# One rotary rotation for queries and keys of a head, with the projections reordered and the reciprocals in PSUM

## The chip, the cores and the metric

The kernel runs on one core of a Trainium2 chip. The time is device microseconds (us) from launch to end of one execution. Three runs of the kernel before took 1827.94 to 1831.23 us, median 1830.76. The profile shown is of a further execution, of 1832.47 us; its span from the first to the last instruction is 1830.7 us. Times of day below are us from the start of that span. Engines: PE (TensorE), PEld (its weight loads), ACT (ScalarE), DVE (VectorE), POOL (GpSimd) and SP (SyncE), which here issues the DMAs of the attention stage.

## What is computed

A language-model block on 8 sequences (batches) of 512 tokens, 64 channels: token embedding with layer norm, attention with 16 heads, then a mixture of 8 experts. The change lies in the attention. Per batch and head:

```python
q  = concat([cq @ Wq_nope, rope(cq @ Wq_rope)])        # 512 queries; 64 of the columns are rotated
o1 = attn(q, k1, v1, causal)                           # compressed keys, the same rotation for all heads
ks = concat([sel @ Wsel_k[:, :32], rope(sel @ Wsel_k[:, 32:])])   # 128 selected tokens
o2 = attn(q, ks, vs)
kw = concat([x @ Wwin_k[:, :32], rope(x @ Wwin_k[:, 32:])])       # 512 tokens, window of 128
o3 = attn(q, kw, vw, window)
o  = g[0] * o1 + g[1] * o2 + g[2] * o3                 # then o @ Wproj
rope(x) = concat([xr * c - xi * s, xr * s + xi * c])   # xr, xi: halves of the 64 columns
```

## The kernel before, in words

The 512 tokens of a batch are four tiles of 128 tokens. Heads follow each other: 8 batches of 16, 128 in all. One head is a *turn* of four *units*, one unit for each tile of queries (`turn(...)` in the code of each engine, t = 0 to 3; the text counts the units from first to fourth). The engines run their own programs and meet at semaphores; no planner sets the order, it is written out by hand.

**PE** in unit t of turn h: a projection for a later head, if this unit has one; `scores` (L1356) of the unit three ahead, so that from the second unit on they belong to head h+1; `turn_probs` (L1381, L1388), which transposes the probabilities of the next unit; `values` (L1403) of this unit. The scores of head h+1 begin in the second unit and wait there for that head's transposed keys and queries (`k_turned`, `q_turned`). Projections: `k_proj(h+2)` in the first unit and `q_proj(h+2)` in the second (L1312, L1315, L1303). All projections write the one PSUM bank X, so each waits until ACT has emptied X of the one before (`x_wait`).

**ACT** empties X (`evac_k`, `evac_q`, both recorded at L576) at the head of the same units, then `take_hi` (L647: the high half of the transposed probabilities), then `probs` (L635: the exponentials). It works strictly in that order.

**DVE** takes `maxima` (L1008) and `take_lo` (L1018, the low half) in each unit, and at the end of a turn `combine`: reciprocals of the softmax sums (L1025, `rinv`, in SBUF), their product with the gates (L1027, `coef`), and the product with the branch outputs in PSUM bank O (L1030), which frees O for the values of the next head.

**POOL** prepares a head two ahead (`prepare`): `key` = rotation of 5 tiles of keys (four of the window, one of the selected tokens; 64 columns each) by two products (L424, L425) and a difference and a sum of half as many columns (L428, L429), then the split into a high and a low fp16 part (L457, L460); `query` = the same rotation of the 4 tiles of queries, from the same lines, and the split (L446, L449). A semaphore wait stands between products and difference, and between rotation and split. Then `low_values` (L480) and `branch_sum` (L473, L475) for the heads before. The rotation of the keys waits for `evac_k`, that of the queries for `evac_q`.

**SP** issues for each head the DMA transpose of the keys (L319, `kh<-kparts`) and then that of the queries (L328, `qh<-qparts`), each after its split.

So there is a round over two heads: projection of head h+2 in turn h, ACT, POOL, DMA, its scores in turn h+1, and the projection in turn h+2 after them.

**Between batches** turns 14 and 15 have projections of the next batch instead (the list `LEAD`, also through X), with single rotations on POOL, and `behind` fills the gap before the next batch's first turn: transposes of the attention output (L1479) that need POOL's last `branch_sum`. In turns 0 and 1 PE projects the output of the batch before (`project_rows`, L1416, into X as well) in the third and fourth unit; DVE adds it to the residual (`half_residual`, L1107) in the fourth, and PE waits at the end of the turn for that (`h_done`). In the last batch POOL also normalises rows for the experts in every second turn (`normalise`).

Of the kernel before, what the change touches and what calls it, by code (L numbers as in the profile page):

```python
# [23 lines left out]
K_ID, K_MASK, K_COS, K_SIN, K_IOTA, K_DESC, K_STK, K_END = 0, 128, 384, 704, 1024, 1152, 1164, 1228  # L24
# [8 lines left out]
def tower(nc, d, out):  # L33
# [5 lines left out]
    with ctx:  # L39
# [6 lines left out]
        def sem(name):  # L46
# [5 lines left out]
        cos5 = cst[:, K_COS:K_COS + 5 * ROPE].rearrange("p (t r) -> p t r", t=5)  # L52
# [97 lines left out]
        qs = [sb(f"qs{i}", [P, NT, QW]) for i in range(2)]  # L150
        kk = [sb(f"kk{i}", [P, 5, P]) for i in range(2)]
        work = big[:].rearrange("p a n -> p (a n)")
        NPR, NRT, NOB = 7 * P, 2 * 5 * ROPE, NT * 3 * VD
# [3 lines left out]
        rt = [work[:, 4 * NPR + i * NRT:4 * NPR + (i + 1) * NRT].rearrange("p (a t r) -> p a t r", a=2, t=5)  # L157
              for i in range(2)]
        obr = [work[:, 4 * NPR + 2 * NRT + i * NOB:4 * NPR + 2 * NRT + (i + 1) * NOB].rearrange("p (t k d) -> p t k d", t=NT, k=3)
               for i in range(2)]  # L160
        qparts = sb("qparts", [P, 2, NT, QW], fp16)
# [14 lines left out]
        rinv = sb("rinv", [P, NT, 3])  # L176
# [29 lines left out]
            "x_ready", "x_evac", "rope_tq", "rope_tk", "rope_q", "rope_k",  # L206
# [20 lines left out]
        ZT = PT[:, 7 * P:8 * P]  # L227
        TBANK = [X[0:C, :], S[0][0:C, 0:512]]
# [4 lines left out]
        LEAD = ["cq", "qp0", "sel", "k1", "kp0", "qp1", "kp1"]  # L233
        NX = (NH - 2) * 2 + len(LEAD)

        def x_index(p, kind):
            return 2 * p + ["kp", "qp"].index(kind)
# [130 lines left out]
        def _(g):  # L368
# [52 lines left out]
            def rope(src, tmp, part, done, tiles, n):  # L421

                v = src[:, 0:tiles, NOPE:HD]
                g.tensor_tensor(tmp[:, 0, 0:tiles, :], v, cos5[:, 0:tiles, :], ALU.mult)  # L424
                g.tensor_tensor(tmp[:, 1, 0:tiles, :], v, sin5[:, 0:tiles, :], ALU.mult).then_inc(part, 1)  # L425
                g.wait_ge(part, n)
                hf = ROPE // 2
                g.tensor_tensor(src[:, 0:tiles, NOPE:NOPE + hf], tmp[:, 0, 0:tiles, 0:hf], tmp[:, 1, 0:tiles, hf:ROPE], ALU.subtract)  # L428
                g.tensor_tensor(src[:, 0:tiles, NOPE + hf:HD], tmp[:, 0, 0:tiles, hf:ROPE], tmp[:, 1, 0:tiles, 0:hf], ALU.add).then_inc(done, 1)  # L429

            def rope_q(par, b, hh, x):

                g.wait_ge(s["x_evac"], x + 2)
                rope(qs[par], rt[0], s["rope_tq"], s["rope_q"], NT, b * NH + hh + 1)

            def rope_k(par, b, hh, x):
                g.wait_ge(s["x_evac"], x + 2)
                rope(kk[par], rt[1], s["rope_tk"], s["rope_k"], 5, b * NH + hh + 1)

            def split_query(par, b, hh):  # L440
                H = b * NH + hh
                g.wait_ge(s["rope_q"], H + 1)
# [8 lines left out]
            def split_key(par, b, hh):  # L451
                H = b * NH + hh
                g.wait_ge(s["rope_k"], H + 1)
# [8 lines left out]
            def query(par, b, hh, x):  # L462
                rope_q(par, b, hh, x)
                split_query(par, b, hh)

            def key(par, b, hh, x):
                rope_k(par, b, hh, x)
                split_key(par, b, hh)
# [12 lines left out]

            query(0, 0, 0, xbase(0) + x_lead("qp0"))
# [42 lines left out]
            def prepare(b, h, hh, par, rows=None):  # L525

                x = xbase(b) + h * 2
                key(par, b, hh, x + x_index(0, "kp"))
                query(par, b, hh, x + x_index(0, "qp"))
                if rows is not None:  # L530
                    normalise(rows, xn_b[:])
                low_values(1 - par, b, hh - 1)

            def heads(b, rows=False):
                prepare(b, 0, 2, 0, 0 if rows else None)
                with g.Fori(0, NH // 2 - 2) as hp:
                    prepare(b, hp * 2 + 1, hp * 2 + 3, 1)
                    branch_sum(0, b, hp * 2)
                    prepare(b, hp * 2 + 2, hp * 2 + 4, 0, hp + 1 if rows else None)
                    branch_sum(1, b, hp * 2 + 1)  # L540
                prepare(b, NH - 3, NH - 1, 1)
                branch_sum(0, b, NH - 4)
                branch_sum(1, b, NH - 3)
# [30 lines left out]
        def _(act):  # L574
# [83 lines left out]
            def turn(b, h, xb, p, last, nxt=None, rows=None):  # L658
# [3 lines left out]
                for t in range(NT):  # L662
                    u = p * NT + t
                    if t == 0 and last < 1:
                        evac_k(p, xb + x_index(0, "kp"), H + 1)
                    if t == 1 and last < 1:
# [3 lines left out]
                    if nxt is not None:  # L670
# [25 lines left out]
            def lead(i, nxt, H=None):  # L696
# [9 lines left out]
                elif kind[:2] == "qp":  # L706
                    evac_q(int(kind[2]), x, H)
                elif kind[:2] == "kp":
                    evac_k(int(kind[2]), x, H)

            def behind(b, nxt, U, first):
# [12 lines left out]
                probs(0, 0, b, U)  # L724
                if not first:
# [5 lines left out]
            for i in range(len(LEAD)):  # L731
# [5 lines left out]
            def heads(b, rows=False):  # L737
                with act.Fori(0, NH // 2 - 1) as hp:
                    for p in range(2):
                        turn(b, hp * 2 + p, xbase(b) + hp * 4 + p * 2, p, 0, rows=hp if rows and p == 1 else None)  # L740

# [53 lines left out]
        def _(dve):  # L795
# [225 lines left out]
            def combine(par, b, H):  # L1021
# [87 lines left out]
            def turn(b, H, p, last, nxt=None, rows=None, back=None):  # L1109

                U = H * NT
                for t in range(NT):
# [11 lines left out]
                    if back is not None and t == 3:  # L1124
# [105 lines left out]
        def _(pe):  # L1230
# [189 lines left out]
            def turn(h, H, xb, p, last, b=None, nxt=None, rows=None, back=None):  # L1420
# [3 lines left out]
                for t in range(NT):  # L1424
                    u = p * NT + t
                    if last < 1 and t == 0:
                        k_proj(h + 2, xb + x_index(0, "kp"))
                    if last < 1 and t == 1:
                        q_proj(h + 2, xb + x_index(0, "qp"))
                    if back is not None and t >= 2:  # L1430
                        project_rows(back, p * 2 + t - 2, xb + 2)
                    i = t if last == 1 else t + 4
                    if nxt is not None and i < len(LEAD):
# [15 lines left out]
                if back is not None:  # L1449
                    pe.wait_ge(s["h_done"], back * 2 + p + 1)  # L1450
# [21 lines left out]
            def behind(b, nxt, H, first):  # L1472
# [20 lines left out]
                scores(0, 0, 0, H * NT)  # L1493
                if not first:
# [19 lines left out]
            def heads(b, rows=False):  # L1514
                for p in range(2):
                    turn(p, b * NH + p, xbase(b) + p * 2, p, 0, rows=0 if rows and p == 1 else None, back=b - 1 if b > 0 else None)
                with pe.Fori(1, NH // 2 - 1) as hp:
                    for p in range(2):
                        turn(hp * 2 + p, b * NH + hp * 2 + p, xbase(b) + hp * 4 + p * 2, p, 0,
                             rows=hp if rows and p == 1 else None)  # L1520

# [20 lines left out]
            for kind in LEAD[2:]:  # L1542
# [130 lines left out]
def _constants():  # L1673
# [9 lines left out]
    for col, tab in ((K_COS, np.cos(ang)), (K_SIN, np.sin(ang))):  # L1683
        for t in range(5):
# [33 lines left out]
```

## Time and profile before

| | busy us | share of the span |
|---|---|---|
| PE | 1423.3 | 78% |
| PEld | 1150.3 | 63% |
| DVE | 1436.5 | 78% |
| ACT | 1225.4 | 67% |
| POOL | 1437.0 | 78% |
| span | 1830.7 | |
| this execution | 1832.47 | |
| median of three others | 1830.76 | |

The shares are means over the whole span. The first 230 us or so prepare embeddings and weights, the attention turns fill the stretch to 1751 us, and the experts the rest. TensorE's granted clock is at full speed (0.96 to 1.00) through the turns. A wait is put down to the semaphore that came last.

### The profile page before, as it was taken

The numbers are of one execution on the slowest core, as the hardware profiler recorded it, in microseconds if no ns is written. First come the engines' busy times: TensorE is split into PE (matmuls) and PEld (weight loads), VectorE is DVE, ScalarE is ACT, GpSimd is POOL, SyncE is SP. The second block draws the span as 40 slices with busy tenths as digits, with TensorE's granted clock in tenths as the row PEclk, the third lists the DMA queues.
The fourth block names the chain that finished last, engine by engine and source line by source line (L and its number), as shares of the span: only waits on it lengthen the run. The fifth ranks groups of instructions, "written<-read, shape, count | busy, mean of one in ns | idle before, by whom it ended". The sixth has DMA issues, their size and how long they took to land.

```text
span 1830.7 us, 62295 instructions
## 1 busy us (share of the span) xinstructions
PE 1423.3 (78%) x19368; PEld 1150.3 (63%) x19368; DVE 1436.5 (78%) x4989; ACT 1225.4 (67%) x3280; POOL 1437.0 (78%) x2126
## 2 busy tenths in 40 slices
PE   1041488888888888888888888888888888888778
PEld 0021377767777777777777776777767776766643
DVE  5747678887888788878887888888887888778845
ACT  0041277777777787778877777777767877777644
POOL 6775489877887899789987889788878997899610
PEclk9985699999999999999999999999999999999989
DMA  5110132223222322232222222222222222323200
GB/s 93 22 26 2 35 71 57 52 45 64 52 52 45 71 52 56 46 64 52 53 51 64 53 52 57 56 53 52 55 60 53 52 56 42 60 62 69 54 4 20
DMA packets 327634, 93.11 MB, mean 51 GB/s; under 512 B 321104, under 2 KB 323024, under 8 KB 327520
## 3 DMA queue, kind: packets, MB, share of 16 engines
q1 hardware_dynamic: 324448, 88.48, 24.9%
q0 software_dynamic: 3072, 3.15, 0.9%
q8 instruction: 66, 1.08, 0.2%
q14 instruction: 48, 0.39, 0.1%
HBM read 6.51 MB, written 1.05 MB: 4 GB/s over the span
## 4 chain that ended last, share of the span: by engine, by line
POOL 60%; issue 17%; DVE 10%; PE 8%; POOLq 2%; DMA 2%; ACT 1%; DVEq 0%; ACTq 0%; SPq 0%
POOL big L425 9%; POOL big L424 9%; POOL kparts L460 7%; POOL big L394 5%; POOL vh L480 4%; POOL qparts L446 4%; POOL kparts L457 4%; POOL kk L428 3%; POOL kk L429 3%; POOL qs L428 3%; POOL qs L429 3%; DVE S L1008 3%; POOL osum L473 2%; POOL qparts L449 1%; PE S L1356 1%
## 5 line engine op out<-in xcount | busy, mean ns | idle before, releaser
L635 ACT ACTIVATE big<-S,negm 128x128 f32<-128x128 f32 (+3 forms) x1536 | 577.4, 450 | 196.8 <-DVE negm L1008 195.7
L647 ACT ACTIVATE big<-PT 128x384 f16<-128x384 f32 (+3 forms) x1024 | 426.6, 455 | 150.7 <-PE PT L1381 112.2
L1018 DVE SCALAR_TENSOR_TENSOR big<-PT,big 128x384 f16<-128x384 f32 (+3 forms) x1024 | 472.1, 500 | 39.1 <-ACT big L647 26.3
L1008 DVE CUSTOM_DVE_ANT_0 S<-S,mask_c,unscale 128x128 f32<-128x128 f32 (+3 forms) x512 | 285.1, 557 | 182.8 <-PE S L1356 176.6
L1356 PE MATMUL S<-k1T,qh 128*128 128x128 f16 (+3 forms) x1536 | 296.8, 302 | 113.9 <-DMA qh<-qparts 98.0
L1356 PE MATMUL S<-kh,qh 128*128 128x128 f16 (+1 forms) x3072 | 323.3, 242 | 0.0
L1403 PEld LDWEIGHTS O<-vh,big 128*128 128x128 f16 x8064 | 272.7, 96 | 41.9 <-issue 14.3
L1403 PE MATMUL O<-vh,big 128*128 128x33 f16 x8064 | 283.3, 178 | 14.7 <-DVE big L1030 8.0
L1356 PEld LDWEIGHTS S<-kh,qh 128*128 128x128 f16 x3072 | 229.9, 99 | 56.0
L1388 PE MATMUL PT<-cst,big 128*128 128x128 f32 x1408 | 248.6, 281 | 16.8 <-DVE big L1018 15.1
L1381 PE MATMUL PT<-cst,big 128*128 128x128 f32 x1280 | 232.6, 281 | 19.1 <-DVE big L1018 17.4
L1008 DVE CUSTOM_DVE_ANT_0 S<-S,cst,kfix 128x256 f32<-128x256 f32 (+1 forms) x512 | 232.5, 454 | 0.0
L1008 DVE DVE_READ_ACCUMULATOR2_ANT negm<- 128x1 f32 x1536 | 217.0, 141 | 0.2
L1356 PEld LDWEIGHTS S<-k1T,qh 128*128 128x128 f16 x1536 | 113.4, 99 | 160.9 <-issue 109.4
L1388 PEld LDWEIGHTS PT<-cst,big 128*128 128x128 f32 x1408 | 162.9, 144 | 47.1 <-issue 40.8
L1008 DVE CUSTOM_DVE_ANT_0 S<-S,mask_c,kfix 128x128 f32<-128x128 f32 x512 | 181.4, 354 | 0.1
L1381 PEld LDWEIGHTS PT<-cst,big 128*128 128x128 f32 x1280 | 153.0, 144 | 38.2 <-DVE big L1018 19.1
L449 POOL TENSOR_TENSOR qparts<-qs,qparts 128x512 f16<-128x512 f32 x128 | 148.4, 1159 | 18.5
L460 POOL TENSOR_TENSOR kparts<-kk,kparts 128x480 f16<-128x480 f32 x128 | 140.9, 1101 | 18.6
L424 POOL TENSOR_TENSOR big<-kk,cst 128x320 f32<-128x320 f32 x128 | 110.3, 862 | 47.0 <-ACT kk L576 46.6
L1303 PE MATMUL X<-wqh,cqT 128*128 (+1 forms) x1536 | 114.5, 222 | 17.9 <-DVE cqT L960 14.8
L424 POOL TENSOR_TENSOR big<-qs,cst 128x256 f32<-128x256 f32 x128 | 93.7, 732 | 29.1 <-ACT qs L576 29.1
(298 smaller groups left out, 2399.7 us busy)
## 6 DMA issues: line engine op xcount, KB each, us to landing
lat_b<-lat_all SPq DMA_DIRECT2D x8, 448.0 KB, 3.1
qh<-qparts SPq DMA_TRANSPOSE x128, 3.0
kh<-kparts SPq DMA_TRANSPOSE x128, 3.4
xnT_all<-xnT_b SPq DMA_DIRECT2D x14, 128.0 KB, 2.5
xn_b<-xn_all SPq DMA_DIRECT2D x8, 128.0 KB, 2.9
xnT_b<-xnT_all SPq DMA_DIRECT2D x8, 128.0 KB, 2.4
out_dram<-h_all SPq DMA_DIRECT2D x8, 128.0 KB, 2.0
xn_all<-xn_b SPq DMA_DIRECT2D x7, 128.0 KB, 2.0
```

Source lines behind the costliest of these rows:

```text
L424: g.tensor_tensor(tmp[:, 0, 0:tiles, :], v, cos5[:, 0:tiles, :], ALU.mult)
L425: g.tensor_tensor(tmp[:, 1, 0:tiles, :], v, sin5[:, 0:tiles, :], ALU.mult).then_inc(part, 1)
L449: g.tensor_tensor(qparts[:, 1], qs[par][:], qparts[:, 0], ALU.subtract).then_inc(s["q_split"], 1)
L460: g.tensor_tensor(kparts[:, 1, :, NOPE:P], kk[par][:, :, NOPE:P], kparts[:, 0, :, NOPE:P], ALU.subtract).then_inc(s["k_split"], 1)
L635: last = nc.scalar.activation(pr[par][:, lo:lo + n], S[par][:, lo:lo + n], ACT.Exp, bias=negm[par][:, k:k + 1], scale=-1.0)
L647: last = nc.scalar.activation(pT[par][:, 0, lo:lo + n], PT[:, lo:lo + n], ACT.Copy, scale=PSCALE)
L1008: last = v.tensor_tensor_reduce(out=z, in0=z, in1=m, scale=unscale[:] if k == 0 else kfix[:], scalar=3.0e38, op0=ALU.add, op1=ALU.min, acc ...
L1018: v.scalar_tensor_tensor(pT[par][:, 1, lo:lo + n], PT[:, lo:lo + n], PSCALE, pT[par][:, 0, lo:lo + n], ALU.mult, ALU.subtract).then_inc(s[ ...
L1356: last = mm(z[:, lo:lo + n], qh[par][:, c, t * P:(t + 1) * P], keys[:, a, :], start=(c + a == 0), stop=(c == 1))
L1381: last = tp(PT[:, lo:lo + P], src[:, lo:lo + P], ident)
L1388: last = tp(PT[:, lo:lo + P], src[:, lo:lo + P], ident)
L1403: last = mm(o, w[:, c, blocks[i] * P:(blocks[i] + 1) * P], vh[p][:, a, v0 + i, :], start=(j == 0), stop=(j == len(parts) - 1))
```

## The change

The rotation of queries and keys of one head becomes one rotation of nine tiles. For that, the two live side by side (`qk`), the cosine table in the constants grows from five to nine tiles, and POOL copies a nine-tile sine table once at its start (two copies). PE projects the queries of head h+2 in the first unit of turn h and the keys of head h+3 in its fourth; the keys of head 2 of a batch come in `behind` (`kp2`, after the first scores). POOL waits for the queries alone before a head's rotation. ACT empties X in the same units. `project_rows` moves from the third and fourth to the second and third unit, `half_residual` to the third, and PE's wait for it ahead of the projection in the fourth. DVE writes the reciprocals into the free end of PSUM bank O. SP's program is not changed.

```diff
-K_ID, K_MASK, K_COS, K_SIN, K_IOTA, K_DESC, K_STK, K_END = 0, 128, 384, 704, 1024, 1152, 1164, 1228
+K_ID, K_MASK, K_COS, K_SIN, K_IOTA, K_DESC, K_STK, K_END = 0, 128, 384, 960, 1280, 1408, 1420, 1484
...
+        qk = [sb(f"qk{i}", [P, NT + 5, P]) for i in range(2)]
+        qs, kk = [q[:, 0:NT] for q in qk], [q[:, NT:NT + 5] for q in qk]
...
-        rinv = sb("rinv", [P, NT, 3])
+        rinv = O[:, NT * 3 * (VD + 1):NT * 3 * (VD + 2)]
...
-        LEAD = ["cq", "qp0", "sel", "k1", "kp0", "qp1", "kp1"]
+        LEAD = ["cq", "qp0", "sel", "k1", "kp0", "qp1", "kp1", "kp2"]
...
+            g.tensor_copy(sin9[:, 0:NT], sin5[:, 0:NT]).then_inc(s["sin_ready"], 1)
+            g.tensor_copy(sin9[:, NT:NT + 5], sin5).then_inc(s["sin_ready"], 1)
+            def rope(src, tmp, cos, sin, n):
+                v, hf = src[:, :, NOPE:HD], ROPE // 2
+                g.tensor_tensor(tmp[:, 0], v, cos, ALU.mult)
+                g.tensor_tensor(tmp[:, 1], v, sin, ALU.mult).then_inc(s["rope_t"], 1)
+                g.wait_ge(s["rope_t"], n)
+                g.tensor_tensor(src[:, :, NOPE:NOPE + hf], tmp[:, 0, :, 0:hf], tmp[:, 1, :, hf:ROPE], ALU.subtract)
+                g.tensor_tensor(src[:, :, NOPE + hf:HD], tmp[:, 0, :, hf:ROPE], tmp[:, 1, :, 0:hf], ALU.add).then_inc(s["rope"], 1)
...
-            def prepare(b, h, hh, par, rows=None):
-                x = xbase(b) + h * 2
-                key(par, b, hh, x + x_index(0, "kp"))
-                query(par, b, hh, x + x_index(0, "qp"))
+            def prepare(par, b, hh, x):
+                n = rope_count(b, hh, None)
+                g.wait_ge(s["x_evac"], x + 2)
+                rope(qk[par], rt9, cos9, sin9, n)
+                split_key(par, b, hh, n)
+                split_query(par, b, hh, n)
...
@@ ACT, turn @@
                     if t == 0 and last < 1:
-                        evac_k(p, xb + x_index(0, "kp"), H + 1)
-                    if t == 1 and last < 1:
                         evac_q(p, xb + x_index(0, "qp"), H + 1)
                     if t == 2 and last < 2:
                         high_values(1 - p, b, h + 1)
+                    if t == 3 and last < 1 and more:
+                        evac_k(1 - p, xb + x_index(0, "kp"), H + 2)
...
@@ ACT, behind @@
                 probs(0, 0, b, U)
+                lead(LEAD.index("kp2"), nxt, b * NH)
...
@@ DVE, combine @@
-                v.reciprocal(rinv[:].rearrange("p t k -> p (t k)").unsqueeze(2), o3[:, :, VD:VD + 1]).then_inc(s["coef_chain"], 1)
+                v.reciprocal(rinv.unsqueeze(2), o3[:, :, VD:VD + 1]).then_inc(s["coef_chain"], 1)
...
-                v.tensor_tensor(coef[:], rinv[:], bc(gate_all[:, ds(b, 1), :], [P, NT, 3]), ALU.mult).then_inc(s["coef_chain"], 1)
+                v.tensor_tensor(coef[:], rinv.rearrange("p (t k) -> p t k", k=3), bc(gate_all[:, ds(b, 1), :], [P, NT, 3]), ALU.mult).then_inc(s["coef_chain"], 1)
...
@@ DVE, turn @@
-                    if back is not None and t == 3:
+                    if back is not None and t == 2:
                         half_residual(back, p)
...
@@ PE, turn @@
                     if last < 1 and t == 0:
-                        k_proj(h + 2, xb + x_index(0, "kp"))
-                    if last < 1 and t == 1:
                         q_proj(h + 2, xb + x_index(0, "qp"))
-                    if back is not None and t >= 2:
-                        project_rows(back, p * 2 + t - 2, xb + 2)
+                    if back is not None and t in (1, 2):
+                        project_rows(back, p * 2 + t - 1, xb + 1)
+                    if back is not None and t == 3:
+                        pe.wait_ge(s["h_done"], back * 2 + p + 1)
+                    if last < 1 and t == 3 and more:
+                        k_proj(h + 3, xb + x_index(0, "kp"))
...
-                if back is not None:
-                    pe.wait_ge(s["h_done"], back * 2 + p + 1)
...
@@ PE, behind @@
                 scores(0, 0, 0, H * NT)
+                lead("kp2", b, nxt)
```

## Rows read from the trace of the kernel before

**Rows 1.** The page: the chain that ended last, by engine.
```profile
POOL 60%; issue 17%; DVE 10%; PE 8%; POOLq 2%; DMA 2%; ACT 1%; DVEq 0%; ACTq 0%; SPq 0%
```

**Rows 2.** Stretches: length, busy us of PE, PEld, DVE, ACT, POOL; clock, DMA.
```profile
264.02:384.46 120.44, 104.05 (x1560) 87.24 (x1558) 103.39 (x387) 96.69 (x255) 108.02 (x164) 0.99 0.27 52
...
1397.94:1519.71 121.77, 103.48 (x1558) 87.11 (x1556) 103.16 (x386) 96.63 (x255) 108.30 (x165) 0.99 0.28 54
1590.04:1724.06 134.02, 111.71 (x1629) 94.81 (x1629) 107.40 (x426) 97.91 (x278) 121.21 (x186) 0.99 0.32 63
```

**Rows 3.** Waits, 643.34 to 763.53 us: who for whom, total us, times, longest.
```profile
PE S L1356 <- DMA qh<-qparts: 14.2, 11, 1.4
...
POOL kparts L457 <- POOL kk L429: 2.8, 11, 0.3
```

**Rows 4.** Timeline, POOL, one head: start, us, instruction, [idle before <- releaser].
```profile
687.69 0.86 POOL L424 TENSOR_TENSOR big<-kk,cst 128x320 f32<-128x320 f32 x1
...
695.06 0.61 POOL L446 CAST qparts<-qs 128x512 f16<-128x512 f32 x1 [0.19 <-POOL qs L429]
695.82 1.16 POOL L449 TENSOR_TENSOR qparts<-qs,qparts 128x512 f16<-128x512 f32 x1
...
698.25 0.46 POOL L475 TENSOR_TENSOR o_b<-osum,big 128x128 f32 x1 [0.18 <-POOL osum L473]
698.66 0.86 POOL L424 TENSOR_TENSOR big<-kk,cst 128x320 f32<-128x320 f32 x1
```

**Rows 5.** Waits, 794 to 824 us (turns 0 and 1 of one batch).
```profile
POOL big L424 <- ACT kk L576: 5.3, 3, 2.6
...
PE X L1312 <- DVE h_all L1107: 2.2, 2, 1.3
```

**Rows 6.** Waits, 763 to 798 us (the edge between two batches).
```profile
POOL osum L473 <- DVE big L1030: 4.0, 1, 4.0
...
PE PT L1479 <- POOL o_b L475: 1.4, 1, 1.4
```

**Rows 7.** Groups by shape, POOL, whole run: count, busy us, mean ns, idle before.
```profile
L425 POOL TENSOR_TENSOR big<-kk,cst 128x320 f32<-128x320 f32 x128 | 110.4, 862 | 0.0
...
L425 POOL TENSOR_TENSOR big<-qs,cst 128x256 f32<-128x256 f32 x128 | 93.8, 733 | 0.0
...
L428 POOL TENSOR_TENSOR kk<-big 128x160 f32<-128x160 f32 x128 | 67.6, 528 | 10.0
...
L428 POOL TENSOR_TENSOR qs<-big 128x128 f32<-128x128 f32 x128 | 58.7, 458 | 10.0
```

**Rows 8.** Timeline, PE, the same head.
```profile
689.45 0.34 PE L1356 MATMUL S<-k1T,qh 128*128 128x128 f16 x3 [1.39 <-DMA qh<-qparts]
...
695.56 0.59 PE L1312 MATMUL X<-wkw,xh 128*128 x8
...
696.08 0.81 PE L1356 MATMUL S<-k1T,qh 128*128 128x512 f16 x3
...
698.15 0.91 PE L1303 MATMUL X<-wqh,cqT 128*128 x12
700.37 0.34 PE L1356 MATMUL S<-k1T,qh 128*128 128x128 f16 x3 [1.31 <-DMA qh<-qparts]
```

**Rows 9.** Timeline, ACT, the same head.
```profile
695.83 1.21 ACT L635 ACTIVATE big<-S,negm 128x384 f32<-128x384 f32 x3 [0.34 <-DVE negm L1008]
696.92 0.58 ACT L576 ACTIVATE kk<-X 128x480 f32<-128x480 f32 x1
```

**Rows 10.** The page: DMA issues, count, KB each, median us to landing.
```profile
lat_b<-lat_all SPq DMA_DIRECT2D x8, 448.0 KB, 3.1
qh<-qparts SPq DMA_TRANSPOSE x128, 3.0
kh<-kparts SPq DMA_TRANSPOSE x128, 3.4
```

**Rows 11.** DVE, lines L1027 and L1030, whole run: ns min/median/max.
```profile
L1027 DVE TENSOR_TENSOR coef<-rinv,gate_all x128: 170/602/739, 239.5 to 1750.5; 128x12 f32<-128x12 f32 x128
...
L1030 DVE TENSOR_TENSOR big<-O,coef x128: 556/558/560, 239.7 to 1750.7; 128x384 f32<-128x384 f32 x128
```

More of the change, by code:

```diff
@@ L656, in take_hi, with turn @@
                     last.then_inc(s["pT_hi"], 1)
-            def turn(b, h, xb, p, last, nxt=None, rows=None):
+            def turn(b, h, xb, p, last, nxt=None, rows=None, more=True):
                 H = b * NH + h
@@ L669, in turn @@
                         high_values(1 - p, b, h + 1)
-                    if nxt is not None:
+                    if t == 3 and last < 1 and more:
+                        evac_k(1 - p, xb + x_index(0, "kp"), H + 2)
+                    if nxt is not None and (last == 1 or t < 3):
                         lead(t if last == 1 else t + 4, nxt, b * NH + NH)
@@ L729, in behind @@
                 probs(2, 2, b, U + 2)
-            for i in range(len(LEAD)):
+            for i in range(LEAD.index("kp2")):
                 lead(i, 0)
@@ L737, in heads @@
             def heads(b, rows=False):
-                with act.Fori(0, NH // 2 - 1) as hp:
+                with act.Fori(0, NH // 2 - 2) as hp:
                     for p in range(2):
                         turn(b, hp * 2 + p, xbase(b) + hp * 4 + p * 2, p, 0, rows=hp if rows and p == 1 else None)
+                for p in range(2):
+                    turn(b, NH - 4 + p, xbase(b) + (NH - 4 + p) * 2, p, 0, rows=NH // 2 - 2 if rows and p == 1 else None, more=p == 0)
             def last_heads(b, nxt):
@@ L1418, in project_rows, with turn @@
                     last.then_inc(s["attn_psum"], 1)
-            def turn(h, H, xb, p, last, b=None, nxt=None, rows=None, back=None):
+            def turn(h, H, xb, p, last, b=None, nxt=None, rows=None, back=None, more=True):
                 U = H * NT
@@ L1516, in heads @@
                     turn(p, b * NH + p, xbase(b) + p * 2, p, 0, rows=0 if rows and p == 1 else None, back=b - 1 if b > 0 else None)
-                with pe.Fori(1, NH // 2 - 1) as hp:
+                with pe.Fori(1, NH // 2 - 2) as hp:
                     for p in range(2):
@@ L1520, in heads @@
                              rows=hp if rows and p == 1 else None)
+                for p in range(2):
+                    turn(NH - 4 + p, b * NH + NH - 4 + p, xbase(b) + (NH - 4 + p) * 2, p, 0,
+                         rows=NH // 2 - 2 if rows and p == 1 else None, more=p == 0)
             def hidden(b, chunks=(0, 1, 2, 3), between=None):
@@ L1541, in _ @@
             last.then_inc(s["rank_psum"], 1)
-            for kind in LEAD[2:]:
+            for kind in LEAD[2:LEAD.index("kp2")]:
                 lead(kind, 0, 0)
@@ L1682, in _constants @@
     ang = np.outer(np.arange(T, dtype=np.float32), f)
-    for col, tab in ((K_COS, np.cos(ang)), (K_SIN, np.sin(ang))):
-        for t in range(5):
+    for col, tab, n in ((K_COS, np.cos(ang), 9), (K_SIN, np.sin(ang), 5)):
+        for t in range(n):
             rows = tab[(t % NT) * P:(t % NT) * P + P]
```

73 lines of the change are left out of this document (36 added, 37 removed).

## The prediction

> **What bounds the kernel now.** I began with the chain of waits that ended last: 60% of it is POOL [rows 1], though POOL's busy share of the span is no larger than DVE's. Next I read the stretches. In each of the first seven batches eleven head periods, from the `combine` of head 2 to that of head 13, make one stretch; the seven sum to 846.7 us for 77 heads (first and last are shown), 11.00 us each; the last batch needs 134.02/11 = 12.18 [rows 2]. In these stretches POOL is busy for 108 of 120 us, and its waits are for nothing but itself (0.25 us a head between rotation and split), while PE stands 14.2 us in 11 heads waiting for transposed queries [rows 3]. So POOL runs its list without a pause, 698.66 - 687.69 = 10.97 us a head [rows 4], and the others follow. In the last batch POOL's busy share is as high [rows 2], with normalisations on top. It is otherwise in turns 0 and 1 of a batch, where POOL waits 5.3 us for the keys, and PE 2.2 us for the residual [rows 5], and at the edge between batches, where POOL waits for `combine` and PE for POOL's sum [rows 6].
>
> **POOL's list.** The rotation is eight instructions a head: two products of 862 ns and two halves of 528 for the keys, two of 733 and two of 458 for the queries [rows 7], 5.16 us. A fifth tile costs 862 - 733 = 129 ns in a product and 528 - 458 = 70 in a half [rows 7], so by extrapolation nine tiles take 862 + 4 x 129 = 1378 and 528 + 4 x 70 = 808 ns; two of each are 4.37 us, 0.79 less. Two waits go as well: 0.19 us ahead of the split of the queries [rows 4] and 10.0/128 = 0.08 ahead of their halves [rows 7]. Against that, three starts vanish that overlapped their predecessor by 0.05 us (698.25 + 0.46 against 698.66 [rows 4]). Saved: 0.79 + 0.27 - 0.15 = 0.91; the list takes 10.06 us.
>
> No row has nine tiles, so both ends: if the cost is proportional to tiles, 9/5 x 862 = 1552 and 9/5 x 528 = 950, 5.00 us, and the list takes 10.69. If it follows the widest subtraction, 512 columns in 1.16 us [rows 4], 576 take 1.31 us, and the list takes 9.9. I take 10.06, since two sizes of the very same instruction are the nearest rows.
>
> **The round over two heads.** It must also fit. From the first scores of a head to the next projection's evacuation today: 689.45 [rows 8] to 696.92 + 0.58 [rows 9], 8.05 us. The keys' projection now stands in the fourth unit ahead of its scores, 696.08 - 695.56 = 0.52 us [rows 8]; part of that PE delay is not felt, because ACT reaches the evacuation only after exponentials that wait for DVE anyway [rows 9]. Bounds 0 and 0.52; I take 0.4: 8.45. POOL, from the first product to the end of the queries' split: 695.82 + 1.16 - 687.69 = 9.29 [rows 4], less 0.91, 8.38. From there over the DMA to the scores 700.37 - 696.98 = 3.39 [rows 4, 8]. The round is 20.22 us, 10.11 a head: as long as POOL's list. The keys' DMA was issued some 4.3 us ahead of the queries', and will be some 3 ahead; a landing takes 3.4 us [rows 10], so it is about over when the queries' begins; if one had to wait for the rest of the other, 0.4 us a round, 0.2 a head.
>
> Today's heads take 0.03 us more than POOL's list (11.00 against 10.97); with the same on the longer of the two rounds I take 10.15. **Term 1:** 77 x (11.00 - 10.15) = 65 us.
>
> **Third ring.** Without the wait for the queries PE's turn takes 700.37 - 1.31 - 689.45 = 9.61 us [rows 8]; that is the ring of PE, ACT and DVE over the probabilities. It hides two edits. The evacuation of the keys, 0.58 us [rows 9], moves ahead of `take_hi` in the fourth unit, and the projection of 0.52 ahead of the scores there; if both lie on the ring in full it is 10.71. The reciprocals in PSUM: `coef` takes 602 ns in the median and 170 at least, while the product with an operand in PSUM and one in SBUF has 556 to 560 in all 128 cases [rows 11]. So `coef`, both of whose operands are in SBUF, is held up, beside a POOL that is nearly always busy. I expect about 0.2 after the change, but cost it at nothing, because PE's wait for the queries covers DVE; without that cover it is worth 0.43 us a head.
>
> **Term 2, the last batch:** POOL's list is the bound there with normalisations that stay; 0.9 x 11 = 10 us.
>
> **Term 3, turns 0 and 1:** the residual is added one unit earlier and PE has the transposes and values of the third unit to do until it is there. Of 2.2 us of waits a batch [rows 5] I let 0.5 stay: 1.7 x 7 = 12 us; bounds 0 and 2.2 x 7 = 15. Once this goes, POOL's rotation is late next there.
>
> **At nothing:** head 2's keys in `behind` put 0.58 us of evacuation [rows 9] between ACT's copies; the chain there runs over POOL's `branch_sum` and single rotations [rows 6], which stay; uncovered, 0.58 x 7 = 4 us. SP's two DMAs a head stay in their order; kept in the same queue, they are only issued closer together. The start: two copies of the sine table, at most 0.61 each by the cast of 512 columns [rows 4], and 128 KB more constants, up to 3.1 x 128/448 = 0.9 us [rows 10]; I take 1 of 0 to 2.
>
> **Sum:** 65 + 10 + 12 - 1 = 86 us. The profiled execution took 1832.47 us (span 1830.7 and 1.8 around it), 1.7 above the median of the runs shown; 1832.5 - 86 = 1746.5, or **1745** against the median 1830.8. The low end: list 9.9 and round with it 9.95, 77 x 1.05 + 12 + 15 = 108, 1723.
>
> **Rivals.**
> (a) *The ring becomes the bound*, at 10.71: 77 x 0.29 + 3 in the last batch + 12 = 37, **1794**. For it: PE waits for the queries only 1.3 of 10.97 us, and evacuation and projection move into the unit where ACT already waits for DVE [rows 9]. Against: the queries' evacuation and projection leave the second unit, so the ring's total work is the same. 15%, with what lies between.
> (b) *Fewer instructions save little*: proportional cost, list 10.69, 77 x 0.31 + 0.28 x 11 + 12 = 39, **1792**. Against it: 129 ns a tile leave 862 - 5 x 129 = 217 ns that no tile accounts for [rows 7]. 7%. The Trainium skill (GPSIMD Engine Reference, Instruction dispatch) speaks for this rival: it puts the call of an instruction's routine at tens of cycles only. By that rule the 0.79 would be nearer 0.2 (an estimate: four calls of tens of cycles); the two widths here disagree with it.
> (c) *Slower*: the ring at ACT's fourth unit. `evac_k` waits there for a projection that PE reaches only after `values`, and `take_hi` and `probs` are queued behind it; DVE's `maxima` and PE's scores wait for those. 10.71, and if `coef` goes on waiting, now for products of 1.38 instead of 0.86 us, 0.52 more: 11.23, 77 x 0.23 = 18, with turns 0 and 1 unchanged **1849**. It decides once the ring passes 11.00. Against it stand the constant 558 ns of the mixed product [rows 11]. 7%. The Trainium skill (SBUF — State Buffer, Who interferes with whom) has a rule against it: a DVE instruction with at most one SBUF input, outside the two-port modes, doesn't contend with GpSimd. By it (c) ends at 10.71, which is (a); the trace agrees as far as those 128 cases go.
> (d) *No change*: the ring at 11.0, or `coef`'s wait and the DMAs' closeness eating the rest. The reciprocals' part then does not do what it is written for. 3%.
>
> **How the numbers follow.** My forecast, rounds of 10.0 to 10.4, has 68%: 1723 to 1770. With (a) and (b) added up to 1796, 90%. The range is 1723 to 1796; outside lie (c), (d) and a bit below. A change of 0.2%, 3.7 us, is about what a measurement of this kernel can tell from none. Faster 0.90, same 0.03, slower 0.07.
>
> **What would show it.** POOL's products at 128x576 with a mean near 1.38 us and halves at 128x288 near 0.81; the stretches of eleven heads near 112 us; `coef` near 0.2 us; the wait of PE for the residual gone from turns 0 and 1; PE's wait for the queries still there, since POOL or the round stays the bound. If that wait is gone and PE, ACT and DVE wait for each other, (a) holds. If products come near 1.55, (b). If a first unit of a turn finds PE waiting for X, (c). A stretch of over 121 us would make the forecast wrong in sign.

## The result and the profile after

The changed kernel takes **1754.67 us** (median of four runs, 1751.09 to 1758.25) against 1830.51 before (four runs, 1827.94 to 1831.23): ratio 0.959, 95% interval 0.9578 to 0.9602, 75.8 us less. Forecast were 1745 and 86 us less, with a range of 1723 to 1796. The profiled execution has a span of 1752.5 us. In experiments 1, 3 and 5 below one or two executions ran at a lower clock and took 2 to 3% longer (1800.45; 1870.17; 1779.25 and 1780.57 us); no trace of theirs is kept, and ratios and intervals leave them out.

The page, busy time and the chain that ended last:

```profile
PE 1365.7 (78%) x19368; PEld 1140.4 (65%) x19368; DVE 1399.5 (80%) x4989; ACT 1209.9 (69%) x3280; POOL 1362.3 (78%) x1680
...
POOL 51%; issue 23%; DVE 10%; PE 9%; DMA 3%; POOLq 2%; ACT 2%; DVEq 0%; ACTq 0%; SPq 0%
```

POOL loses 75 us of work, and its share of the chain falls from 60% to 51% [rows 1]. POOL's groups by shape, the rotation:

```profile
L438 POOL TENSOR_TENSOR big<-qk,big 128x576 f32<-128x576 f32 x112 | 157.8, 1409 | 0.0
L437 POOL TENSOR_TENSOR big<-qk,cst 128x576 f32<-128x576 f32 x112 | 156.9, 1401 | 68.3 <-ACT qk L594 66.5 <-issue 0.4 <-POOL pairsel L580 0.2
...
L441 POOL TENSOR_TENSOR qk<-big 128x288 f32<-128x288 f32 x112 | 89.2, 797 | 0.0
L440 POOL TENSOR_TENSOR qk<-big 128x288 f32<-128x288 f32 x112 | 89.1, 795 | 8.8
```

These four instructions replace the eight of [rows 7]: a product takes 1.40 us (forecast 1.38), a half 0.80 (0.81). DVE, the two products of `combine`, ns min/median/max [rows 11]:

```profile
L1048 DVE TENSOR_TENSOR coef<-O,gate_all x128: 169/171/172, 237.8 to 1671.8; 128x12 f32<-128x12 f32 x128
...
L1051 DVE TENSOR_TENSOR big<-O,coef x128: 556/557/559, 238.1 to 1672.0; 128x384 f32<-128x384 f32 x128
```

`coef` fell from 602 to 171 ns. The stretches from the `combine` of head 2 to that of head 13 (length; busy us of PE, PEld, DVE, ACT, POOL; clock, DMA), batches 0, 2, 5, 6 and the last:

```profile
261.32:373.83 112.51, 96.63 (x1544) 84.90 (x1543) 98.51 (x387) 94.18 (x253) 101.16 (x120) 1.00 0.30 56
619.50:731.52 112.02, 95.72 (x1545) 84.81 (x1544) 98.70 (x386) 94.17 (x253) 101.65 (x121) 1.00 0.31 58
1156.18:1271.93 115.75, 97.29 (x1544) 86.08 (x1543) 98.79 (x387) 94.35 (x253) 101.65 (x122) 0.99 0.32 57
1337.37:1452.39 115.02, 97.31 (x1544) 86.00 (x1543) 98.82 (x386) 94.40 (x253) 101.97 (x122) 0.99 0.33 57
1521.33:1645.13 123.80, 107.75 (x1619) 92.00 (x1617) 105.30 (x427) 96.66 (x277) 114.04 (x143) 1.00 0.33 67
```

Against [rows 2]: the seven stretches sum to 795.9 instead of 846.7 us (50.8 less), the last one has 10.2 less. The rest of the 78.2 us by which the span fell: the seven edges between them 479.3 to 464.1 (15.2), the start up to head 2 264.02 to 261.32 (2.7), and the tail 0.7 more. Batches 2 and 3 run at 112.0, 10.18 us a head; batches 5 and 6 need 3 to 4 us more. Waits in the stretch of batch 2 (total us, times, longest):

```profile
PE S L1377 <- DMA qh<-qparts: 12.7, 9, 1.8
...
POOL big L437 <- ACT qk L594: 1.4, 5, 0.4
```

PE still waits for the queries [rows 3], and POOL now at times for the evacuated queries: both the list and the round are near the pace.

**Where the slower batches lose.** It is mostly one head in each, head 3, which takes 13.3 to 13.7 us in batches 1, 5 and 6 and 12.1 in batch 4, against 10.5 to 10.6 in batches 2 and 3. PE's timeline in batch 1 (the last line is from batch 2), then the stretches of batch 1 with its wait and with what follows:

```profile
439.28 0.39 PE L1424 MATMUL O<-vh,big 128*128 128x33 f16 x9
442.76 0.34 PE L1377 MATMUL S<-k1T,qh 128*128 128x128 f16 x3 [3.08 <-DMA qh<-qparts]
...
446.01 1.06 PE L1402 MATMUL PT<-cst,big 128*128 128x128 f32 x4
...
613.60 0.60 PE L1402 MATMUL PT<-cst,big 128*128 128x128 f32 x4
```

```profile
440.00:442.70 2.70, 0.00 (x0) 0.00 (x0) 1.36 (x6) 1.48 (x4) 2.62 (x3) 1.00 0.86 96
443.90:447.30 3.40, 3.40 (x33) 3.01 (x32) 2.45 (x13) 2.12 (x7) 2.83 (x5) 0.51 0.00 0
447.30:450.70 3.40, 3.27 (x66) 2.86 (x66) 2.49 (x9) 2.89 (x8) 2.42 (x4) 1.00 1.12 139
```

PE stands idle for 3.08 us; about a microsecond after it resumes, its granted clock is 0.51, the lower level (1.2 GHz), and four transposes of probabilities (L1402) take 1.06 us where batch 2, at full clock, needs 0.60. Batches 4, 5 and 6 show the same behind waits of 1.99, 3.60 and 3.22 us. In three of the four, transposes had landed late ahead of the wait: in batch 1 the queries' 3.8 us after issue, in batch 5 the queries' 4.7, in batch 6 the keys' 5.3 and the queries' 4.4 (medians 3.5 for keys, 3.1 for queries). In batch 4 both were on time (3.6 and 3.1), and the wait was hardly longer than the 1.8 us at the same place in batches 2 and 3, where the clock stayed up. Why it fell in batch 4 stays open, but the batch shows what the clock alone costs. Heads 3 and 4 of batch 2, then of batch 4:

```profile
619.49:630.07 10.58, 8.66 (x141) 7.56 (x140) 8.93 (x36) 8.67 (x24) 9.66 (x12) 1.00 0.34 66
630.07:640.13 10.06, 9.13 (x148) 8.03 (x145) 9.07 (x37) 8.58 (x24) 8.87 (x11) 1.00 0.26 50
...
976.57:988.69 12.12, 10.01 (x141) 8.74 (x140) 9.31 (x36) 8.63 (x24) 9.68 (x13) 0.86 0.38 74
988.69:998.74 10.05, 9.35 (x148) 8.00 (x145) 8.97 (x36) 8.64 (x24) 8.86 (x11) 1.00 0.17 33
```

That is 1.5 us, and the next head doesn't give it back. Head 3 loses some 10 us in the four batches together; by this estimate four times 1.5, some 6 us, is the clock's, and the rest the late landings'.

### The profile page after: what moved, and what is told of

Its sections match the earlier page's. It is cut to its first block, busy times and chain, and to the rows that moved or that the text cites. A ratio compares the mean times of both kernels' runs of the same rounds, so it can differ in the third digit from the quotient of the medians.

```text
span 1752.5 us, 61262 instructions
## 1 busy us (share of the span) xinstructions
PE 1365.7 (78%) x19368; PEld 1140.4 (65%) x19368; DVE 1399.5 (80%) x4989; ACT 1209.9 (69%) x3280; POOL 1362.3 (78%) x1680
## 4 chain that ended last, share of the span: by engine, by line
POOL 51%; issue 23%; DVE 10%; PE 9%; DMA 3%; POOLq 2%; ACT 2%; DVEq 0%; ACTq 0%; SPq 0%
POOL big L438 9%; POOL big L437 8%; POOL big L398 6%; POOL qk L440 5%; POOL qk L441 5%; POOL vh L492 4%; POOL kparts L469 4%; POOL qparts L458 4%; DVE S L1029 3%; POOL osum L485 2%; PE S L1377 2%; DMA kh<-kparts 2%; POOL o_b L487 2%; DVE big L1039 1%; POOL kparts L472 1%
## 5 line engine op out<-in xcount | busy, mean ns | idle before, releaser
L665 ACT ACTIVATE big<-PT 128x384 f16<-128x384 f32 (+3 forms) x1024 | 417.3, 458 | 90.1 <-PE PT L1402 67.6
L437 POOL TENSOR_TENSOR big<-qk,cst 128x576 f32<-128x576 f32 (+2 forms) x144 | 182.5, 1267 | 104.9 <-ACT qk L594 103.1
L1409 PE MATMUL PT<-cst,big 128*128 128x128 f32 x1408 | 244.5, 278 | 2.7 <-DVE big L1039 2.6
L1402 PE MATMUL PT<-cst,big 128*128 128x128 f32 x1280 | 230.7, 279 | 17.0 <-DVE big L1039 16.4
L1402 PEld LDWEIGHTS PT<-cst,big 128*128 128x128 f32 x1280 | 151.4, 143 | 32.0 <-issue 14.7
L461 POOL TENSOR_TENSOR qparts<-qk,qparts 128x512 f16<-128x512 f32 x128 | 148.2, 1158 | 18.6
L594 ACT ACTIVATE qk<-X 128x480 f32<-128x480 f32 (+1 forms) x256 | 151.8, 593 | 14.5 <-PE X L1324 11.3
L438 POOL TENSOR_TENSOR big<-qk,big 128x576 f32<-128x576 f32 x112 | 157.8, 1409 | 0.0
L472 POOL TENSOR_TENSOR kparts<-qk,kparts 128x480 f16<-128x480 f32 x128 | 140.5, 1097 | 18.6
```

What stands on the lines that cost most here:

```text
L437: g.tensor_tensor(tmp[:, 0], v, cos, ALU.mult)
L438: g.tensor_tensor(tmp[:, 1], v, sin, ALU.mult).then_inc(s["rope_t"], 1)
L472: g.tensor_tensor(kparts[:, 1, :, NOPE:P], kk[par][:, :, NOPE:P], kparts[:, 0, :, NOPE:P], ALU.subtract).then_inc(s["k_split"], 1)
L594: return nc.scalar.activation(dst, src, ACT.Copy)
L665: last = nc.scalar.activation(pT[par][:, 0, lo:lo + n], PT[:, lo:lo + n], ACT.Copy, scale=PSCALE)
L1402: last = tp(PT[:, lo:lo + P], src[:, lo:lo + P], ident)
```

## The experiments

**1. The reciprocals alone, both ways.** First undone in the changed kernel:

```diff
+        rinv = sb("rinv", [P, NT, 3])
...
-        rinv = O[:, NT * 3 * (VD + 1):NT * 3 * (VD + 2)]
...
```

Expected: 

> The changed kernel with the reciprocals back in SBUF and nothing else undone. In the changed kernel coef takes 171 ns in all 128 cases, before it took 602 in the median. Theory: coef goes back to 0.4 to 0.6 us, but PE waits some 1.2 us a head for the transposed queries, which covers DVE; the time stays within 6 us of 1754.7 (1753 to 1761). Rival: the ring of PE, ACT and DVE is the bound by now, and the 0.43 us come out in full: 77 x 0.43 = 33 in the stretches and some 5 in the last batch, 1793.

Measured: 1759.61 us, ratio to before 0.9599 (0.9579 to 0.9618), against 0.959 (0.9578 to 0.9602) for the changed kernel: not to be told apart. The rival's 33 us did not come, but `coef` came back only in part, 221 ns in the median and 311 in the mean (sum 39.8 us over 128), so the test put back less than was meant. What it did put back is covered: in batches 2 and 3, at full clock in both kernels, `coef` takes 3.3 us over the eleven heads instead of 1.9, yet the stretches last 112.10 and 111.95 us against 112.02 and 111.93. Batch 2 and `coef` in this kernel:

```profile
622.38:734.48 112.10, 96.34 (x1544) 84.86 (x1544) 100.02 (x386) 94.27 (x254) 101.84 (x122) 1.00 0.31 58
...
L1048 DVE TENSOR_TENSOR coef<-rinv,gate_all x128: 170/221/777, 237.0 to 1677.7; 128x12 f32<-128x12 f32 x128
```

Then done alone in the kernel before (the same lines the other way round). Expected: 

> The kernel before with the reciprocals in PSUM and nothing else changed. coef falls from 0.6 to 0.17 us. Theory: POOL's list sets the pace and PE's wait for queries covers DVE: no difference beyond 4 us, 1826 to 1834. Rival: combine comes 0.43 us earlier and branch_sum, the edges and the last batch gain by it: 1815 to 1825.

Measured: 1830.42 us, ratio 1.000 (0.9991 to 1.001), with `coef` at 171 ns. In either kernel the reciprocals' place has no measurable effect.

**2. The rotation undone.** Keys and queries rotated one after the other, all else as changed:

```diff
...
-                rope(qk[par], rt9, cos9, sin9, n)
+                rope(kk[par], rt[1], cos5, sin5, n)
                 split_key(par, b, hh, n)
-                split_query(par, b, hh, n)
+                rope(qs[par], rt[0], cos5[:, 0:NT], sin5[:, 0:NT], n + 1)
+                split_query(par, b, hh, n + 1)
```

Expected: 

> The changed kernel with one rotation for the keys and one for the queries in each head (eight instructions instead of four); projections, evacuations and everything else stay as changed. Theory: the gain is that of POOL's list; the list goes from 10.03 back to some 10.95 us a head, the eleven-head stretches from 113.7 back to 120 to 121 (77 x 0.63 = 49 us), the last batch loses its 10 and head 2 of each batch some 8: 1815 to 1828. Rival: the gain came from the queries' projection being one unit earlier, so that less than a third of the 76 us is lost: below 1780.

Measured: 1839.81 us, 85 more than the changed kernel and **slower than the kernel before**: ratio 1.005 (1.0034 to 1.0067). Without the joint rotation nothing of the gain is left, and the rival (an earlier projection) is out. But the time lies 12 us over the theory's range. The stretch of batch 2 in the kernel before and here, and PE's timeline here:

```profile
643.34:763.53 120.19, 101.92 (x1558) 85.97 (x1556) 103.92 (x387) 96.59 (x255) 108.43 (x165) 1.00 0.28 54
...
642.75:765.63 122.88, 102.07 (x1545) 88.47 (x1544) 99.05 (x386) 94.74 (x253) 108.53 (x166) 0.96 0.28 53
```

```profile
679.52 0.34 PE L1378 MATMUL S<-k1T,qh 128*128 128x128 f16 x3 [1.95 <-DMA qh<-qparts]
...
690.51 0.34 PE L1378 MATMUL S<-k1T,qh 128*128 128x128 f16 x3 [2.25 <-DMA qh<-qparts]
```

The new order makes PE wait about 2 us in eight of these eleven heads where the kernel before waited 1.3 [rows 8], and the clock over the whole stretch is 0.96 instead of 1.00: in every third or fourth head it falls to its lower level behind such a wait, and that head takes some 12.5 us.

**3. The wait filled.** The same kernel with PE busy in that place:

```diff
+                        if t == 1 and last < 1 and more:
+                            for i in range(16):
+                                mm(O[:, 412:508], xh[:, 0:P], wkw[:, 0, 0, :], start=True, stop=True)
                         if t == 1:
                             pe.wait_ge(s["k_turned"], H * 16 + 48)
```

Expected: 

> The kernel with two rotations a head, in which PE now fills its wait: 16 matmuls of 96 columns into free columns of PSUM bank O, whose results nobody reads, ahead of the wait for the transposed keys and queries in the second unit of heads 0 to 12 (about 1 us of work where PE otherwise stands idle for 2.0 to 2.25 us a head). Theory: TensorE's clock falls to its lower level behind those long waits, and that is why this kernel took 1839.8 and not 1815 to 1828; with the waits cut in two the low-clock stretches (33 of 3.4 us or longer in the profile) become fewer than 10 and the time falls to 1812 to 1830. Rival: the low clock has another cause, the stretches stay (25 or more) and the time is 1836 to 1850.

Measured: 1828.03 us, ratio 0.999 (0.998 to 1.000), 12 less with 1664 matmuls more. In the profile 10 stretches of low clock are left of 34 (between 220 and 1760 us), and batch 2 runs at full clock:

```profile
637.69:758.31 120.62, 103.15 (x1705) 91.47 (x1704) 98.65 (x386) 94.75 (x253) 108.67 (x166) 1.00 0.30 54
```

Most waits are 1.3 to 1.5 us in this stretch now. So it is PE's standing idle there that brings most of the low clock. The length of one wait does not decide it alone. In heads 3 to 14 of the kernel before, 66 waits ahead of a head's first scores took 1.2 to 1.45 us, and the clock fell behind six of them; in the changed kernel it fell behind none of 47 waits of 1.2 to 1.75 us and five of 13 longer ones; in experiment 2 behind 28 of 61 waits over 1.75 us. The same filling in the changed kernel takes 8 matmuls. Expected: 

> The changed kernel with 8 such filling matmuls (about 0.5 us) at the same place; PE's wait there is about 1.2 us a head, so that they cost nothing in an undisturbed head. Theory: the waits of 2 to 3.6 us at head 3 get 0.5 us shorter, so some of the five low-clock stretches between the first scores and the last batch's end go: 1742 to 1755. Rival: unchanged, 1751 to 1760, as the longest waits stay over 2 us.

Measured: 1756.08 us, ratio 0.9605 (0.9589 to 0.9621), as the rival had it. Five low-clock stretches stand between 240 and 1620 us, as many as without the filling; the waits ahead of them are still 2.0 to 2.9 us.

**4. Which of the two bounds sets the pace.** POOL's list shortened behind the queries' split, so that the round keeps its length:

```diff
...
-                g.tensor_tensor(vh[par][:, 1, :, 0:VD], vall[:, :, ds(hh * VD, VD)], vh[par][:, 0, :, 0:VD], ALU.subtract)
+                g.tensor_tensor(vh[par][:, 1, :, 0:2], vall[:, :, ds(hh * VD, 2)], vh[par][:, 0, :, 0:2], ALU.subtract)
```

Expected: 

> The changed kernel in which POOL makes the low half of the values for 2 of the 32 columns only; the low half of the other 30 columns is left out (zero), so the time is that of a POOL list shorter by some 0.48 us (0.715 against 0.23 of a very small instruction) in every head, with the round over two heads as it was, since this instruction stands behind the queries' split. Theory: the round of 20.2 to 20.4 us binds nearly as tightly as the list, so little is gained: heads go from 10.18 to 10.1 at best in undisturbed batches, 0 to 10 us in all, 1745 to 1755. Rival: POOL's list alone is the bound, and 0.48 x 77 + 5 = 42 us go: 1713.

Measured: 1747.68 us, ratio 0.9549 (0.9533 to 0.9565). The instruction takes 243 instead of 715 ns, yet the stretch of batch 2 keeps its 112 us, and POOL's wait for the queries grows from 1.4 to 6.3 us:

```profile
617.87:729.80 111.93, 95.56 (x1544) 84.83 (x1543) 98.66 (x387) 93.92 (x253) 96.51 (x122) 1.00 0.31 58
```

```profile
POOL big L437 <- ACT qk L594: 6.3, 11, 0.9
```

So in the seven batches it is the **round over two heads** that sets the changed kernel's pace. What was gained lies elsewhere: 4.5 us in the last batch, where POOL normalises too (123.8 to 119.3), and 3.4 at the edges between batches, by the profile, whose execution was the fastest of the four (1741.92 us).

**5. The round shortened.** Two ways. PE projects the queries a unit earlier, ahead of `values`, and ACT empties them ahead of the exponentials:

```diff
...
+                    if t == 3 and last < 1 and more:
+                        evac_q(1 - p, xb + 2 + x_index(0, "qp"), H + 2)
                     if last < 2 or t < 1:
                         probs(u + 3, (t + 3) % NT, b, U + t + 3)
...
+                    if last < 1 and t == 3 and more:
+                        q_proj(h + 3, xb + 2 + x_index(0, "qp"))
                     values(u, t, p, U + t, H)
```

Expected: 

> The changed kernel with the queries' projection moved from the first unit of a turn to the fourth of the turn before, behind the keys' projection and ahead of values; ACT empties it ahead of the exponentials of that unit, where it now waits 0.82 us for DVE. Only the first turn of a batch keeps its place. POOL's list is unchanged; the round over two heads gets shorter by about 0.9 us. Theory: with the round at 19.4 the list of 10.03 us alone sets the pace, PE's waits for queries get shorter, and the low-clock stretches behind the waits of 2 to 3.6 us at head 3 go too: the seven stretches from 795.9 to 77 x 10.05 = 774, 22 us less, 1725 to 1740. Rival 1: the list was the bound already and the low-clock stretches have another cause: 1750 to 1756. Rival 2: values come 0.8 us later, combine with them, and the ring of PE, ACT and DVE (9.6) grows over 10.2: slower, 1760 to 1790.

Measured: 1732.03 and 1740.27 us in two executions, too few for a ratio; the profile is that of 1732.03. In it the seven stretches sum to 781.2, without low clock, and a new bound shows, waits in batch 2:

```profile
PEld PT L1406 <- DVE big L1043: 6.8, 9, 0.9
ACT qk L594 <- PE X L1328: 6.6, 10, 0.7
...
PE S L1381 <- DMA qh<-qparts: 0.5, 2, 0.3
```

PE no longer waits for queries; PE, ACT and DVE wait for each other at 10.12 us a head. That is the prediction's rival (a) in another kernel. The second way leaves PE's order alone and takes only ACT's edit (the first half of the diff; the first pair of turns of a batch is written out for it, since the first turn keeps its place). Expected: 

> The changed kernel with PE's order as changed, and on ACT alone the evacuation of the queries moved ahead of the exponentials of the unit before (where ACT waits 0.82 us for DVE); those exponentials come some 0.5 us later. The round over two heads gets about 1.1 us shorter, POOL's list stays. Theory: the waits of PE for queries nearly go, with them the low-clock stretches, and the list of 10.03 binds: seven stretches of 110.5 to 111.5 against a sum of 795.9, 15 to 22 us less, 1730 to 1742. Rival: the later exponentials hold up PE's transposes and the ring of PE, ACT and DVE passes 10.2: 1745 to 1765.

Measured: **1733.15 us**, ratio 0.9472 (0.9455 to 0.9489), 21.5 less than the changed kernel. POOL's timeline in batch 2:

```profile
640.45 1.41 POOL L437 TENSOR_TENSOR big<-qk,cst 128x576 f32<-128x576 f32 x1
...
650.49 1.40 POOL L437 TENSOR_TENSOR big<-qk,cst 128x576 f32<-128x576 f32 x1
...
660.53 1.41 POOL L437 TENSOR_TENSOR big<-qk,cst 128x576 f32<-128x576 f32 x1
```

POOL runs its list without a pause, 10.04 us a head; the seven stretches sum to 774.0.

**6. One product of 18 tiles** in place of two, with the sine and the cosine table side by side in the constants, alone and with ACT's edit:

```diff
...
-                g.tensor_tensor(tmp[:, 0], v, cos, ALU.mult)
-                g.tensor_tensor(tmp[:, 1], v, sin, ALU.mult).then_inc(s["rope_t"], 1)
+                g.tensor_tensor(tmp, v.unsqueeze(1).to_broadcast([P, 2, NT + 5, ROPE]), table9, ALU.mult).then_inc(s["rope_t"], 1)
...
```

Expected of it alone: 

> The changed kernel with the two products of a rotation in one instruction over 18 tiles (sine and cosine table side by side in the constants, 128 KB more of them; k1n moves into free space of the work tile). By 129 ns a tile and 217 ns a start one instruction takes 2.54 us against 2 x 1.40 less an overlap of 0.05: POOL's list gets 0.2 us shorter, the round over two heads 0.2, so 0.1 a head. Theory: 10.18 to 10.08 in undisturbed heads, 77 x 0.1 = 8, and 2 in the last batch; 1740 to 1752. Rival 1: by a cost proportional to elements it changes nothing, 1751 to 1760. Rival 2: POOL's list is the bound, 77 x 0.2 + 2 = 17, 1735.

Measured: 1747.63 us, ratio 0.9544 (0.9514 to 0.9574), 7 less.

```profile
L436 POOL TENSOR_TENSOR big<-qk,cst 128x1152 f32<-128x1152 f32 x112 | 294.0, 2625 | 74.0 <-ACT qk L594 71.8 <-POOL pairsel L580 0.2
```

With both edits, expected: 

> Both together: the queries emptied ahead of the exponentials and one product of 18 tiles. Theory: POOL's list 9.83, round 19.0, ring 9.6 to 9.9; heads of 9.85 to 9.95, the seven stretches 109 each, 1712 to 1728. Rival: the ring of PE, ACT and DVE is at 10.1 to 10.2 as in the kernel with the early projection, and nothing is added to the early evacuation alone: 1730 to 1742.

Measured: **1719.92 us** (1719.15 to 1722.04), ratio 0.9404 (0.9386 to 0.9422). This version beats both kernels, the changed one by 35 us. Its stretch of batch 2, 9.88 us a head:

```profile
610.07:718.74 108.67, 100.04 (x1545) 84.63 (x1544) 98.36 (x387) 92.37 (x253) 99.42 (x110) 1.00 0.32 61
```

**7. Late transposes and the fetch of code.** PE's loop over the middle heads written out:

```diff
-                with pe.Fori(1, NH // 2 - 2) as hp:
+                for hp in range(1, NH // 2 - 2):
```

Expected: 

> The changed kernel in which PE's loop over the middle heads of a batch is written out (the same instructions in the same order, but every head's code is fetched anew). In the trace of the changed kernel all 37 transposes that landed over 3.75 us after issue overlapped a fetch of instructions, and none of the 192 without a fetch did; fetches come only at the edges of batches, 85 in all. Theory: the fetches delay the transposes, and PE's wait for them brings the low clock. With fetches in all heads (over 130) late transposes spread over the batch (over 60), the low-clock stretches become more (over 10) and the time rises to 1770 to 1830. Rival: the late transposes come from the other traffic at the edges (latents, rows) and stay there; the time stays at 1750 to 1760.

Measured: 1754.41 us, ratio 0.9596 (0.9575 to 0.9617). The first half of the theory holds, the second does not. From the page, the larger of the two queues of instructions (packets, MB, share), 85 packets in the changed kernel:

```profile
q8 instruction: 158, 2.59, 0.6%
```

| transposes, landing over 3.75 us | beside a fetch of code | without one |
|---|---|---|
| kernel before | 13 of 53 | 0 of 203 |
| changed kernel | 37 of 64 | 0 of 192 |
| PE's loop written out | 61 of 115 | 0 of 141 |
| two rotations (experiment 2) | 15 of 61 | 0 of 195 |

With nearly twice the fetches there are 61 late transposes and 8 low-clock stretches instead of 5 between 240 and 1620 us, now in the middle of batches too, and still the time is the same: the seven stretches sum to 795.1. That transposes land late beside a fetch of code, and follow the fetches when these move, is shown; that the fetches are what the slower batches cost is not. The last row adds something: that kernel has as many fetches as the changed one (85 packets), but issues the keys' transpose 4.3 us ahead of the queries', as the kernel before does, and a quarter of its transposes beside a fetch are late in place of more than half. A late transpose can cost where PE is already waiting for it, and head 3 of a batch is such a place.

## Why the prediction was right, and where it was not

**Bound and list: right.** POOL's list was forecast at 10.06 us and takes 10.04 where it runs unhindered (experiment 5). The rounds of 20.22 us were forecast as long as the list; they take 2 x 10.18 = 20.36 and are the tighter of the two (experiment 4). The three parts are as forecast, too. One round in batch 2, its scores, the queries' evacuation, the end of their split, and the next scores:

```profile
621.74 0.34 PE L1377 MATMUL S<-k1T,qh 128*128 128x128 f16 x3 [1.79 <-DMA qh<-qparts]
...
629.76 0.60 ACT L594 ACTIVATE qk<-X 128x512 f32<-128x512 f32 x1
...
637.64 1.16 POOL L461 TENSOR_TENSOR qparts<-qk,qparts 128x512 f16<-128x512 f32 x1
...
642.27 0.34 PE L1377 MATMUL S<-k1T,qh 128*128 128x128 f16 x3 [1.69 <-DMA qh<-qparts]
```

That is 8.62, 8.44 and 3.47 us against 8.45, 8.38 and 3.39.

**Term 1: too large, 65 against 50.8 us.** The step that failed is "I take 10.15" for all 77 heads. The undisturbed ones run at 10.18 (77 x 0.03 = 2.3 us). The other 11.9 us, 795.9 - 7 x 112.0, are lost almost wholly in batches 1, 4, 5 and 6, mostly to late transposes and low clock at head 3. I had read PE's wait for the queries as cover only, never as something that slows PE afterwards. In the kernel before there were even more stretches of low clock, 10 between 240 and 1620 us against 5, though over whole stretches the clock reads 0.96 to 1.00, and they cost less, 846.7 - 7 x 120.3 = 4.6 us. Two heads of its batch 0:

```profile
351.24:363.33 12.09, 10.31 (x139) 8.76 (x139) 9.27 (x36) 8.49 (x23) 10.74 (x17) 0.86 0.29 57
363.33:373.54 10.21, 9.67 (x148) 8.00 (x146) 9.11 (x36) 8.57 (x24) 9.10 (x14) 1.00 0.26 48
```

POOL's list ran on meanwhile, and the next head was shorter, so that both together lost 0.4 us against 2 x 10.97. With the round as the bound the next head makes up for nothing (1.5 us lost in batch 4). Shorten the round, and 21.5 us come out (experiment 5), some 11 more than the list alone would give (77 x (10.18 - 10.04) = 10.8).

**Term 2: right**, 10.2 against 10. **Term 3: 12 forecast, 15.2 measured.** Five edges without low clock in experiment 2, with the early residual and the old list, take 66.1 to 66.6 us against 67.8 to 68.1 before, which is the 1.7 of the term, though the new order of projections is in it; in the changed kernel five take 65.4 to 65.9, and the further 0.7 or so comes with the joint rotation. PE's wait for the residual did not shrink to 0.5. Waits in turns 0 and 1 of the same batch as in [rows 5]:

```profile
POOL big L437 <- ACT qk L594: 6.4, 3, 2.8
...
PE X L1333 <- DVE h_all L1128: 0.9, 2, 0.5
```

As forecast, POOL's rotation is what is late there now. That the early residual alone gives this was not tried.

**At nothing: right for the reciprocals, not for the DMAs.** The reciprocals have no measurable effect in either kernel (experiment 1); `coef` is at 0.17 for a forecast of 0.2. The keys' DMA is issued 1.77 us ahead of the queries', not "some 3": behind the keys' split stands only the queries' own. The median landings of 3.5 and 3.1 us are 0.1 longer [rows 10], but 37 transposes of 256 land late instead of 13, and by the table of experiment 7 that goes with the closeness. The start got 2.7 us shorter where I took 1 longer. No run shows that to be the change's: with the reciprocals alone moved in the kernel before, the start took 259.8 us, with nothing changed 264.0.

**The total is in part luck.** Term 1 was 14.2 us too large; term 3 and the start erred by 3.2 and 3.7 the other way and hid half of it.

**Rivals.** (a) did not come: PE still waits for queries. (b) is refuted by 1.40 us a product. With the three widths 320, 576 and 1152 columns at 862, 1405 and 2625 ns a tile costs 136 ns and an instruction 1405 - 9 x 136 = 181 beside it. The Trainium skill (GPSIMD Engine Reference, Instruction dispatch) has tens of cycles for that call; the measurement decides against reading this as the whole start of an instruction. (c) needed `coef` to go on waiting, and it stopped. The Trainium skill (SBUF — State Buffer, Who interferes with whom) says that a DVE instruction with at most one input in SBUF, outside the two-port modes, doesn't contend with GpSimd; the 169 to 172 ns in all 128 cases agree. (d) did not come either; the time fell by 75.8 us. The one thing that did make a kernel slower than before (experiment 2) is in none of the rivals.

## What to carry to other kernels

When two nearly equal bounds stand behind each other, price both, then ask which gets back what a disturbance costs: here POOL's list, which never pauses, did (0.4 us lost), and the round did not (1.5). Look for the place where an in-order engine already waits (ACT's 0.8 us for DVE) and put the round's next step there; that gave 21.5 us here. And a wait of PE is not free cover: look at the granted clock behind it.

## What had not been expected of the hardware

- In the middle of a steady kernel, behind waits of 2 to 3.6 us, PE's granted clock fell to 0.5 and a head took 12.1 to 13.7 instead of 10.5 us; in the kernel before it fell behind six of 66 waits of 1.2 to 1.45 us. With PE's recurring wait of about 2 us filled by matmuls that nobody reads, 34 such stretches became 10 and the time fell by 12 us.
- In the four profiles of the table no transpose landed over 3.75 us after its issue unless a fetch of instructions ran beside it; the latest took 5.8 us instead of 3.5. Beside a fetch a quarter were late where keys and queries were issued 4.3 us apart, and more than half where they were 1.8 us apart.
- `coef`, with both inputs in SBUF, took 602 ns in the median beside the eight-instruction rotation, 221 beside the joint one, and 171 with one input in PSUM beside either.
